# Windowed channel attention: both gate products of a pair of steps issued together ahead of an even step's value product, one in the pair banks and one in the score banks

## The chip, the cores and the metric

The kernel runs on one core of one Trainium2 chip, in one launch. The metric is device microseconds, the median of three runs. TensorE (PE) does the matrix products, VectorE (DVE) and ScalarE (ACT) read the results from the accumulation memory (PSUM), SyncE issues the transfers. All data are fp32.

## The reference

The input x is (4, 64, 128, 128). It is normalised in groups of two channels, and a block is added to it:

```python
qkv = einsum('bchw,oc->bohw', gn(x), w_qkv) + b_qkv      # 64 -> 192 channels
qkv = depthwise_conv_3x3(qkv, w_dw) + b_dw
# 8x8 windows: q, k, v of shape (windows, 4 heads, 16 channels, 64 pixels)
attn = softmax(einsum('nhcx,nhdx->nhcd', q, k) * temperature, axis=-1)
out  = einsum('nhcd,nhdx->nhcx', attn, v)
gate = gelu(einsum('nhcx,yx->nhcy', v, w_mlp) + b_mlp)
out  = einsum('bchw,oc->bohw', out * gate, w_proj) + b_proj
return x + out
```

Attention is over channels (a 16 x 16 table for each window and head), and the gate is a 64 x 64 product over the pixels of each window of v.

## The kernel before

The four images are two pairs; a pair's 2 x 64 channels fill the 128 partitions. A chunk is a band of 16 rows of one pair, that is 64 windows of 8 x 8 pixels (two rows of 16 windows for two images). There are 16 chunks. A chunk's windows are attended in four batches, so there are 64 steps; `a = i % 4` is the batch of step `i`. Step `i` belongs to chunk `i // 4`, and between its attention products PE does the work that prepares the next chunk, the filler units of `fillers(i)`:

- in a = 0 and a = 1 eight channel units each (`mix_channels`, L674, 8 records of MATMUL for a unit), which take the 10 x 10 patches through `w_qkv`;
- in a = 2 and a = 3 three depthwise units each (`depthwise`, L709, 64 records for a unit), numbered 0 to 5 here, which give q, k and v of 16 channels.

All units go through two PSUM buffers in turn (`work[0]`, `work[1]`, two banks each). ACT copies a unit out (L326), except depthwise unit 1, which DVE copies (L417). A unit can start only when the unit two before it is copied out. An fp32 product is two MATMUL records.

The attention of a step has these parts. On PE: `score` (L747, q times k), `gates` (L763, v times `w_mlp`, for a later step `j`), `turn_v` (L773, the transpose of v), `apply_probs` (L787, the value product), `project` (L796, of the step before). On DVE: `scores_up` (L511 to L518: mask, maximum, shift), `gate_up` (L525, gate product plus bias), `divide` and `turn` (L532 to L543), `mix` (L503, value product times gate), `residual` (L552). On ACT: `exponent` (L341), `v_up` (L347, copy of the transposed v) and `gelu` (L351). Exp and Gelu lie in different ACT tables, so each pair of gelus has a table load ahead of it, and an `exp_table` with another load (L356) behind it. Each engine runs its list in the order in which it is written; there is no scheduler.

The other four PSUM banks are `rest_ps`. `pair_ps` is its first two: the transposed v fills the first, `project` the second, and the value product the first halves of both. `score_ps` is its last two: scores in their first halves, and gate products in the second halves (`gate_ps`).

Before, `gates_in(i)` gives two gates to each odd step and none to an even one but the first. In an odd step one gate stands ahead of `project`, the other between two groups of filler units. `gate_up` of the first comes between `scores_up` and `divide` on DVE, that of the second after `residual`, behind `turn`. ACT's order in a = 3 is `exponent`, copy of unit 3, `v_up`, table load and `gelu`, copy of unit 4, `gelu`, copy of unit 5, `exp_table`. The first score of a chunk waits until units 4 and 5 are copied out (`qkv_of`), since it reads them.

Of the kernel before, what the change touches and what calls it, by code (L numbers as in the profile page):

```python
# [12 lines left out]
B, C, H, W = 4, 64, 128, 128  # L13
HEADS, WS = 4, 8
HW = WS * WS
# [12 lines left out]
BATCH = 4  # L28
BATCHES = COLS // BATCH
STEPS = CHUNKS * BATCHES  # L30
# [12 lines left out]
GATES = 3  # L43
# [42 lines left out]

def gates_in(i):

    return (0, 1) if i == 0 else (i + 1, i + 2) if i % 2 and i + 2 < STEPS else ()


def gelus_in(i):

    a = i % BATCHES
    return (0, 1) if i == 0 else (i, i + 1) if a == 2 else gates_in(i) if a == 3 else ()


def looks_until(i):
# [4 lines left out]
def build(nc, x, taps, hot, edges, weights, out):  # L103
    with ExitStack() as ctx:
# [45 lines left out]
        pair_ps = rest_ps[:, 0:2]  # L150
        turn_ps, proj_ps = pair_ps[:, 0], pair_ps[:, 1]
        score_ps = rest_ps[:, 2:4]
        gate_ps = score_ps[:, :, BATCH * C:]

        x_in = [sem(f"x_in{n}") for n in range(BANDS)]
        x_last = sem("x_last")
# [256 lines left out]
        def _(dve):  # L413
# [91 lines left out]
            def scores_up(i):  # L505

                dve.wait_ge(scores_done, i + 1)
                if i:
                    dve.wait_ge(probs_t_ready, i)
                over = [P, 2, BATCH, C]  # L510
                nc.vector.tensor_tensor(scores[:].rearrange("p (h g) d -> p h g d", h=2),  # L511
                                        score_ps[:, :, 0:BATCH * C].rearrange("p h (g d) -> p h g d", d=C),
                                        other_head.unsqueeze(1).unsqueeze(1).to_broadcast(over),
                                        ALU.add).then_inc(masked, 1)
                dve.wait_ge(masked, i + 1)
                nc.vector.tensor_reduce(neg_max[:], scores[:], AX_X, ALU.max, negate=True).then_inc(max_ready, 1)
                dve.wait_ge(max_ready, i + 1)
                nc.vector.tensor_tensor(scores[:], scores[:], neg_max[:].unsqueeze(2).to_broadcast([P, WIDE, C]),  # L518
                                        ALU.add).then_inc(shifted, 1)

            def gate_up(j):
                dve.wait_ge(gate_done, j + 1)
                if j >= GATES:
                    dve.wait_ge(proj_done, j - GATES + 1)
                nc.vector.tensor_tensor(  # L525
                    gate[:, j % GATES], gate_ps.rearrange("p b (g y) -> p b g y", y=HW),
                    b_mlp.unsqueeze(1).unsqueeze(1).to_broadcast([P, 2, BATCH, HW]), ALU.add).then_inc(gate_biased, 1)

            def divide(i):
# [55 lines left out]
            for i in range(STEPS):  # L585
                n, a = i // BATCHES + 1, i % BATCHES
                if i:
                    mix(i - 1)
                if (n, a) == (BANDS - 1, 1):
                    centre(1)  # L590
                if (n, a) == (BANDS - 1, 2):
                    variance(1)
                scores_up(i)
                now = gates_in(i)
                if now:
                    gate_up(now[0])
                elif i:
                    residual(i - 1)
                divide(i)
                turn(i)  # L600
                if now:
                    if i:
                        residual(i - 1)
                    gate_up(now[1])
                if n < CHUNKS and a == 2:
                    evacuate_dw(dve, copy, n, 1)
                if (n, a) == (BANDS - 1, 2):
                    normaliser(1)
                if a == 2 and n + 1 < CHUNKS:
                    pads(n + 1)  # L610
                    normalise(n + 1, 0)
                if a == 3 and n + 1 < CHUNKS:
                    normalise(n + 1, 1)
                for p in range(looks_until(i), looks_until(i + 1)):
                    look(p)
                if looks_until(i) < STATS <= looks_until(i + 1):
                    aggregate(1)
# [4 lines left out]
        def _(pe):  # L622
# [110 lines left out]
            def side(b, h):  # L733
                return slice((h ^ b) * HW, (h ^ b) * HW + HW)

            def score(i):

                if i:
                    pe.wait_ge(masked, i)
                    pe.wait_ge(gate_biased, max(j for m in range(i) for j in gates_in(m)) + 1)  # L740
                for g in range(BATCH):
                    q, k = windows(i, g)[:, 0], windows(i, g)[:, 1]
                    for b in range(2):
                        pair = slice(b * C, (b + 1) * C)
                        for h in range(2):
                            rows = slice(h * HW, (h + 1) * HW)
                            last = nc.tensor.matmul(score_ps[pair, h, g * C:(g + 1) * C], q[rows, pair], k[rows, pair],  # L747
                                                    start=True, stop=True)
                last.then_inc(scores_done, 1)

            def gates(j, i):

                pe.wait_ge(masked, i + 1)
                if j:
                    pe.wait_ge(gate_biased, j)
                if j // BATCHES > i // BATCHES:
                    wait_free(pe, ("dw", j // BATCHES, 0))
                    wait_free(pe, ("dw", j // BATCHES, 1))
                for g in range(BATCH):
                    for b in range(2):  # L760
                        for h in range(2):
                            rows = slice(h * HW, (h + 1) * HW)
                            last = nc.tensor.matmul(gate_ps[side(b, h), b, g * HW:(g + 1) * HW],  # L763
                                                    windows(j, g)[rows, 2, b * C:(b + 1) * C], mlp[rows],
                                                    start=True, stop=True)
                last.then_inc(gate_done, 1)

            def turn_v(i):

                if i:  # L770
                    pe.wait_ge(mixed_ready, i)
                for g in range(BATCH):
                    last = nc.tensor.transpose(pair_ps[:, 0, g * P:(g + 1) * P], windows(i, g)[:, 2], ident)  # L773
                last.then_inc(v_t_done, 1)

            def apply_probs(i):

                pe.wait_ge(v_t_ready, i + 1)
                pe.wait_ge(probs_t_ready, i + 1)
                if i:  # L780
                    pe.wait_ge(out_ready, i)
                for g in range(BATCH):
                    for h in range(2):
                        at = slice((2 * g + h) * HW, (2 * g + h + 1) * HW)
                        for b in range(2):
                            rows = slice(b * C, (b + 1) * C)
                            last = nc.tensor.matmul(pair_ps[side(b, h), b, g * HW:(g + 1) * HW],  # L787
                                                    probs_t[rows, h * BATCH + g, :], v_t[rows, at],
                                                    start=True, stop=True)
                last.then_inc(mix_done, 1)  # L790

            def project(i):

                pe.wait_ge(mixed_ready, i + 1)
                for b in range(2):
                    last = nc.tensor.matmul(proj_ps[:, b * 4 * HW:(b + 1) * 4 * HW], proj[:, b * P:(b + 1) * P],  # L796
                                            gate[:, i % GATES, b].rearrange("p g (r c) -> p r g c", c=WS),
                                            start=True, stop=True)
                last.then_inc(proj_done, 1)
# [14 lines left out]
                depthwise(0, v)  # L814
            for i in range(STEPS):
                units_now = fillers(i)
                now = gates_in(i)
                cut = (2, 4, 6) if i % BATCHES < 2 else (0, 1, 3) if i % BATCHES == 2 else (1, 2, 3)
                if i % BATCHES == 0:
                    qkv_of(i // BATCHES)  # L820
                if i == 0:
                    fill(units_now[:cut[0]])
                score(i)
                if i:
                    fill(units_now[:cut[0]])
                if now:
                    gates(now[0], i)
                if i:
                    project(i - 1)
                turn_v(i)  # L830
                fill(units_now[cut[0]:cut[1]])
                if now:
                    gates(now[1], i)
                fill(units_now[cut[1]:cut[2]])
                apply_probs(i)
                fill(units_now[cut[2]:])
            project(STEPS - 1)


# [82 lines left out]
```

## Time and profile before

| what | value |
|---|---|
| runs | 676.55, 679.05, 679.55 us; median 679.05 |
| profiled execution | span 680.0 us; no time of its own is given beside it, so it stands 0.95 us above the median |
| PE busy | 625.8 us, 92% of the span |
| DVE, ACT busy | 511.6 us (75%), 482.8 us (71%) |
| mean granted TensorE clock | 0.973 of full speed |

The profile shows one execution. A timeline row gives the start, the length and what an instruction (or a run of equal ones) is; a bracket at its end is the idle time of the engine ahead of it and what ended it. PE's products are pipelined, so a row's length runs into the next row: what a group costs is read from its start to the start of the next. A chunk of the middle takes 38.0 us.

### The profile page before, as it was taken

The page shows a single profiled execution, that of the slowest core. Times are in us where ns is not written, and L with a number is a line of the kernel's source. Part 1 is how long each engine was busy: PE and PEld are TensorE (multiplying, and loading weights), DVE is VectorE, ACT ScalarE, POOL GpSimd, SP SyncE. Part 2 cuts the span into 40 slices and gives each one's busy share as a digit, 9 for nine tenths or more (in the row PEclk, how much of TensorE's full clock was granted, in tenths as well). Part 3 has the DMA queues.
Part 4 walks back from the last instruction along what each step waited for, and adds up shares of the span by engine and source line. Part 5 has one row for each costly group of instructions (what it writes and reads, how often), then busy time and mean ns, then how long its engine had stood idle before and what let it go on. Part 6 is the DMA issues. An engine that isn't in the chain of part 4 may idle for free.

```text
span 680.0 us, 32438 instructions
## 1 busy us (share of the span) xinstructions
PE 625.8 (92%) x15044; PEld 549.1 (81%) x15044; DVE 511.6 (75%) x790; ACT 482.8 (71%) x631; POOL 0.3 (0%) x5
## 2 busy tenths in 40 slices
PE   3788799999999999999999999999999999999954
PEld 2687698888989898888989898888989798888843
DVE  4872688887888888786878676786868676876684
ACT  3652678787877778786877778786877778786722
POOL 0000000000000000000000000000000000000000
PEclk9997899999999999999999999999999999999975
DMA  9872115335171714132050504132150504112022
GB/s 363 263 217 72 33 50 166 110 86 208 33 232 49 234 59 149 66 102 93 8 191 5 195 4 142 60 94 106 29 173 4 198 3 152 44 50 80 4 82 44
DMA packets 29240, 72.28 MB, mean 106 GB/s; under 512 B 9801, under 2 KB 16329, under 8 KB 24233
## 3 DMA queue, kind: packets, MB, share of 16 engines
q1 hardware_dynamic: 28674, 68.57, 31.0%
q8 instruction: 118, 1.93, 1.2%
q10 hardware_dynamic: 432, 1.65, 0.7%
q14 instruction: 16, 0.13, 0.1%
HBM read 53.44 MB, written 16.78 MB: 103 GB/s over the span
## 4 chain that ended last, share of the span: by engine, by line
PE 87%; ACT 5%; DVE 3%; issue 2%; DMA 1%; ACTq 0%; DVEq 0%
PE unit_ps L709 28%; PE unit_ps L674 26%; PE rest_ps L796 10%; PE rest_ps L787 6%; PE rest_ps L763 6%; PE rest_ps L747 6%; PE rest_ps L773 4%; ACT z L326 2%; DMA patches<-in_hot 1%; ACT dw L326 1%; PE rest_ps L643 1%; PE rest_ps L674 1%; PE unit_ps L636 0%; DVE scores L511 0%; DVE scores L536 0%
## 5 line engine op out<-in xcount | busy, mean ns | idle before, releaser
L326 ACT ACTIVATE z<-unit_ps 100x768 f32<-100x768 f32 x244 | 184.9, 808 | 60.1 <-PE unit_ps L674 60.1
L674 PE MATMUL unit_ps<-consts,patches 64*100 64x192 f32 x1984 | 195.0, 336 | 8.6 <-ACT z L326 6.6
L709 PE MATMUL unit_ps<-z,dw 103*64 103x64 f32 (+2 forms) x6144 | 194.3, 224 | 3.0 <-issue 1.7
L709 PEld LDWEIGHTS unit_ps<-z,dw 103*64 103x64 f32 (+2 forms) x6144 | 185.5, 139 | 10.7 <-issue 8.6
L674 PEld LDWEIGHTS unit_ps<-consts,patches 64*100 64x100 f32 x1984 | 153.6, 164 | 25.8 <-ACT z L326 11.2
L326 ACT ACTIVATE qkv<-unit_ps 128x1024 f32<-128x1024 f32 x78 | 79.1, 1014 | 31.5 <-PE unit_ps L709 31.4
L511 DVE TENSOR_TENSOR scores<-rest_ps,consts 128x512 f32<-128x512 f32 x64 | 44.1, 689 | 51.6 <-PE rest_ps L747 51.6
L503 DVE TENSOR_TENSOR gate<-rest_ps,gate 128x512 f32<-128x512 f32 x64 | 44.1, 689 | 47.5 <-PE rest_ps L787 44.6
L796 PE MATMUL rest_ps<-gate,consts 128*128 128x256 f32 x256 | 75.1, 417 | 1.1 <-DVE gate L503 1.0
L347 ACT ACTIVATE v_t<-rest_ps 128x512 f32<-128x512 f32 x64 | 38.2, 597 | 40.5 <-PE rest_ps L773 38.9
L341 ACT ACTIVATE scores<-scores 128x512 f32<-128x512 f32 x64 | 40.4, 631 | 33.2 <-DVE scores L518 31.6
L787 PE MATMUL rest_ps<-v_t,probs_t 64*64 64x64 f32 x2048 | 45.5, 228 | 10.5 <-DVE probs_t L543 10.1
L525 DVE TENSOR_TENSOR gate<-rest_ps,consts 128x512 f32<-128x512 f32 x64 | 44.0, 687 | 14.4 <-PE rest_ps L763 14.0
L796 PEld LDWEIGHTS rest_ps<-gate,consts 128*128 128x128 f32 x256 | 44.9, 195 | 11.9 <-issue 3.5
L747 PE MATMUL rest_ps<-qkv 64*64 64x64 f32 x2048 | 45.4, 227 | 9.0 <-issue 9.0
L787 PEld LDWEIGHTS rest_ps<-v_t,probs_t 64*64 64x64 f32 x2048 | 36.7, 137 | 20.9 <-issue 18.8
L747 PEld LDWEIGHTS rest_ps<-qkv 64*64 64x64 f32 x2048 | 37.9, 138 | 18.1 <-issue 18.1
L552 DVE SCALAR_TENSOR_TENSOR staged<-rest_ps,consts,staged 128x512 f32<-128x512 f32 x64 | 46.7, 729 | 7.5 <-PE rest_ps L796 7.5
L543 DVE STREAM_TRANSPOSE probs_t<-scores 128x512 f32<-128x512 f32 x64 | 45.5, 712 | 2.2
L763 PE MATMUL rest_ps<-consts,qkv 64*64 64x64 f32 x2048 | 45.6, 228 | 1.6 <-DVE scores L511 1.6
L763 PEld LDWEIGHTS rest_ps<-consts,qkv 64*64 64x64 f32 x2048 | 36.7, 138 | 12.3 <-issue 8.2
L518 DVE TENSOR_TENSOR scores<-scores,neg_max 128x512 f32<-128x512 f32 x64 | 44.3, 692 | 2.2
(55 smaller groups left out, 530.5 us busy)
## 6 DMA issues: line engine op xcount, KB each, us to landing
staged<-in_x SPq DMA_DIRECT2D x17, 1024.0 KB, 4.9
out_y<-staged SPq DMA_DIRECT2D x15, 1024.0 KB, 5.4
T<-in_x SPq DMA_DIRECT2D x12, 1152.0 KB, 6.7
seen<-in_x SPq DMA_DIRECT2D x32, 256.0 KB, 2.9
qkv<-in_x SPq DMA_DIRECT2D x6, 1024.0 KB, 13.9
T<-in_x SPq DMA_DIRECT2D x3, 1088.0 KB, 6.7
staged<-in_x SPq DMA_DIRECT2D x2, 512.0 KB, 22.9
out_y<-staged SPq DMA_DIRECT2D x4, 256.0 KB, 3.0
```

What stands on the lines that cost most here:

```text
L326: return nc.scalar.activation(to, of, ACT.Copy)
L503: nc.vector.tensor_tensor(held, pair_ps[:, :, 0:BATCH * HW], held, ALU.mult).then_inc(mixed_ready, 1)
L511: nc.vector.tensor_tensor(scores[:].rearrange("p (h g) d -> p h g d", h=2), score_ps[:, :, 0:BATCH * C].rearrange("p h (g d) -> p h g d", ...
L518: nc.vector.tensor_tensor(scores[:], scores[:], neg_max[:].unsqueeze(2).to_broadcast([P, WIDE, C]), ALU.add).then_inc(shifted, 1)
L543: nc.vector.transpose(probs_t[:].rearrange("p w d -> p (w d)"), scores[:].rearrange("p w d -> p (w d)")).then_inc(probs_t_ready, 1)
L552: nc.vector.scalar_tensor_tensor(to, proj_ps.rearrange("p (r c) -> p r c", r=BAND), b_proj, to, op0=ALU.add, op1=ALU.add).then_inc(out_rea ...
L674: last = nc.tensor.matmul(to[0:NPATCH, t, b * QKV:(b + 1) * QKV], patches[image, b, g], w1[image], start=True, stop=True)
L709: last = nc.tensor.matmul(to[h * HW:(h + 1) * HW, m // 8, m % 8 * NW:(m % 8 + 1) * NW], dw[0:used, c, :], z[0:used, c, :], start=True, sto ...
L747: last = nc.tensor.matmul(score_ps[pair, h, g * C:(g + 1) * C], q[rows, pair], k[rows, pair], start=True, stop=True)
L763: last = nc.tensor.matmul(gate_ps[side(b, h), b, g * HW:(g + 1) * HW], windows(j, g)[rows, 2, b * C:(b + 1) * C], mlp[rows], start=True, s ...
L787: last = nc.tensor.matmul(pair_ps[side(b, h), b, g * HW:(g + 1) * HW], probs_t[rows, h * BATCH + g, :], v_t[rows, at], start=True, stop=True)
L796: last = nc.tensor.matmul(proj_ps[:, b * 4 * HW:(b + 1) * 4 * HW], proj[:, b * P:(b + 1) * P], gate[:, i % GATES, b].rearrange("p g (r c) ...
```

## The change

Each even step `i` gets the gates of steps `i + 2` and `i + 3`, both right ahead of its `apply_probs`; the odd steps get none. The even gate goes to the second halves of the pair banks, the odd one stays in the score banks. In the first step two more gates (0 and 1) stand ahead of its score. DVE keeps its two `gate_up` in the odd step: the first moves ahead of `scores_up`, the second behind `residual` and ahead of `divide`, so `residual` now stands ahead of `divide` in odd steps too. Gelus and copies on ACT stay where they were. Score's halves go to bank `h ^ b` instead of bank `h`, and the value product reads them so. Waits that are new or moved: the even gate waits for `out_ready` and `v_t_ready` of its step, the odd gate for `masked`, `apply_probs` for the even gate's end, `turn_v` and `project` of the next step for the even gate's `gate_up`; `score` no longer waits for `gate_up`.

```diff
 def gates_in(i):
-    return (0, 1) if i == 0 else (i + 1, i + 2) if i % 2 and i + 2 < STEPS else ()
+    return (i + 2, i + 3) if i % 2 == 0 and i + 2 < STEPS else ()

 def gelus_in(i):
     a = i % BATCHES
-    return (0, 1) if i == 0 else (i, i + 1) if a == 2 else gates_in(i) if a == 3 else ()
+    return (0, 1) if i == 0 else (i, i + 1) if a == 2 else gates_in(i - 1) if a == 3 else ()
...
-        gate_ps = score_ps[:, :, BATCH * C:]
+        gate_ps = [pair_ps[:, :, BATCH * HW:], score_ps[:, :, BATCH * C:]]
...
@@ DVE, each step @@
-                scores_up(i)
-                now = gates_in(i)
+                now = gates_in(i - 1) if i else (0, 1)
                 if now:
                     gate_up(now[0])
-                elif i:
+                scores_up(i)
+                if i:
                     residual(i - 1)
+                if now:
+                    gate_up(now[1])
                 divide(i)
                 turn(i)
-                if now:
-                    if i:
-                        residual(i - 1)
-                    gate_up(now[1])
...
@@ PE, score(i) @@
                     pe.wait_ge(masked, i)
-                    pe.wait_ge(gate_biased, max(j for m in range(i) for j in gates_in(m)) + 1)
...
-                            last = nc.tensor.matmul(score_ps[pair, h, g * C:(g + 1) * C], q[rows, pair], k[rows, pair],
+                            last = nc.tensor.matmul(score_ps[pair, h ^ b, g * C:(g + 1) * C], q[rows, pair], k[rows, pair],
...
@@ PE, gates(j, i) @@
-                pe.wait_ge(masked, i + 1)
-                if j:
-                    pe.wait_ge(gate_biased, j)
+                if j > 1:
+                    pe.wait_ge(gate_biased, j - 1)
+                if j % 2 == 0 and i:
+                    pe.wait_ge(out_ready, i)
+                if j % 2 == 0 and j:
+                    pe.wait_ge(v_t_ready, i + 1)
+                if j % 2 and j > 1:
+                    pe.wait_ge(masked, i + 1)
...
-                            last = nc.tensor.matmul(gate_ps[side(b, h), b, g * HW:(g + 1) * HW],
+                            last = nc.tensor.matmul(gate_ps[j % 2][side(b, h), b, g * HW:(g + 1) * HW],
...
@@ PE, turn_v(i) @@
+                for j in gates_in(i - 1)[:1] if i else (0,):
+                    pe.wait_ge(gate_biased, j + 1)
...
@@ PE, apply_probs(i) @@
+                for j in gates_in(i)[:1]:
+                    pe.wait_ge(gate_done, j + 1)
...
-                                                    probs_t[rows, h * BATCH + g, :], v_t[rows, at],
+                                                    probs_t[rows, (h ^ b) * BATCH + g, :], v_t[rows, at],
...
@@ PE, project(i) @@
+                for j in gates_in(i)[:1]:
+                    pe.wait_ge(gate_biased, j + 1)
...
@@ PE, each step @@
-                now = gates_in(i)
-                cut = (2, 4, 6) if i % BATCHES < 2 else (0, 1, 3) if i % BATCHES == 2 else (1, 2, 3)
+                cut = (2, 6) if i % BATCHES < 2 else (i % BATCHES - 2, 3)
...
                 if i == 0:
                     fill(units_now[:cut[0]])
+                    gates(0, 0)
+                    gates(1, 0)
                 score(i)
                 if i:
                     fill(units_now[:cut[0]])
-                if now:
-                    gates(now[0], i)
-                if i:
                     project(i - 1)
                 turn_v(i)
                 fill(units_now[cut[0]:cut[1]])
-                if now:
-                    gates(now[1], i)
-                fill(units_now[cut[1]:cut[2]])
+                for j in gates_in(i):
+                    gates(j, i)
                 apply_probs(i)
-                fill(units_now[cut[2]:])
+                fill(units_now[cut[1]:])
```

## Rows read from the trace of the kernel before

**Rows 1.** The page: the chain that ended last, by engine.
```profile
PE 87%; ACT 5%; DVE 3%; issue 2%; DMA 1%; ACTq 0%; DVEq 0%
```
**Rows 2.** Waits of PE: who for whom, total us, times, longest.
```profile
PE rest_ps L747 <- issue: 9.0, 15, 0.6
PE unit_ps L674 <- ACT z L326: 6.6, 15, 2.9
```
**Rows 3.** Timeline of PE over one chunk: start, length, instructions.
```profile
396.30 0.69 PE L747 MATMUL rest_ps<-qkv 64*64 64x64 f32 x32
...
404.17 0.69 PE L787 MATMUL rest_ps<-v_t,probs_t 64*64 64x64 f32 x32
404.69 0.65 PE L747 MATMUL rest_ps<-qkv 64*64 64x64 f32 x32
...
407.28 0.69 PE L763 MATMUL rest_ps<-consts,qkv 64*64 64x64 f32 x32
407.90 1.13 PE L796 MATMUL rest_ps<-gate,consts 128*128 128x256 f32 x4
...
414.06 0.69 PE L787 MATMUL rest_ps<-v_t,probs_t 64*64 64x64 f32 x32
415.36 0.70 PE L747 MATMUL rest_ps<-qkv 64*64 64x64 f32 x32 [0.61 <-issue]
...
418.96 1.55 PE L674 MATMUL unit_ps<-consts,patches 64*100 64x192 f32 x16
420.77 1.60 PE L674 MATMUL unit_ps<-consts,patches 64*100 64x192 f32 x16 [0.26 <-ACT z L326]
422.29 0.69 PE L787 MATMUL rest_ps<-v_t,probs_t 64*64 64x64 f32 x32
422.92 1.55 PE L674 MATMUL unit_ps<-consts,patches 64*100 64x192 f32 x16
424.40 0.69 PE L747 MATMUL rest_ps<-qkv 64*64 64x64 f32 x32
...
434.30 0.69 PE L747 MATMUL rest_ps<-qkv 64*64 64x64 f32 x32
```
**Rows 4.** Timeline of ACT over the same chunk.
```profile
407.70 0.63 ACT L341 ACTIVATE scores<-scores 128x512 f32<-128x512 f32 x1 [1.17 <-DVE scores L518]
408.24 1.01 ACT L326 ACTIVATE qkv<-unit_ps 128x1024 f32<-128x1024 f32 x1
409.51 0.60 ACT L347 ACTIVATE v_t<-rest_ps 128x512 f32<-128x512 f32 x1 [0.26 <-PE rest_ps L773]
...
411.96 1.01 ACT L326 ACTIVATE qkv<-unit_ps 128x1024 f32<-128x1024 f32 x1
412.90 0.63 ACT L351 ACTIVATE gate<-gate 128x512 f32<-128x512 f32 x1
414.23 1.02 ACT L326 ACTIVATE qkv<-unit_ps 128x1024 f32<-128x1024 f32 x1 [0.70 <-PE unit_ps L709]
...
419.90 1.51 ACT L326 ACTIVATE z<-unit_ps 100x768 f32<-100x768 f32 x2 [0.24 <-PE unit_ps L674]
```
**Rows 5.** Timeline of DVE over the same chunk.
```profile
402.49 1.23 DVE L417 COPY qkv<-unit_ps 128x1024 f32<-128x1024 f32 x1 [0.20 <-PE unit_ps L709]
...
404.93 0.69 DVE L503 TENSOR_TENSOR gate<-rest_ps,gate 128x512 f32<-128x512 f32 x1 [0.20 <-PE rest_ps L787]
405.54 0.68 DVE L511 TENSOR_TENSOR scores<-rest_ps,consts 128x512 f32<-128x512 f32 x1
...
418.63 0.75 DVE L552 SCALAR_TENSOR_TENSOR staged<-rest_ps,consts,staged 128x512 f32<-128x512 f32 x1 [0.38 <-PE rest_ps L796]
...
420.97 0.71 DVE L543 STREAM_TRANSPOSE probs_t<-scores 128x512 f32<-128x512 f32 x1
```
**Rows 6.** Timeline of PE at both ends of the span.
```profile
81.25 1.60 PE L674 MATMUL unit_ps<-consts,patches 64*100 64x192 f32 x16 [2.91 <-ACT z L326]
...
649.81 0.90 PE L787 MATMUL rest_ps<-v_t,probs_t 64*64 64x64 f32 x32 [3.90 <-DVE probs_t L543]
```

More of the change, by code:

```diff
@@ L525, in gate_up @@
                 nc.vector.tensor_tensor(
-                    gate[:, j % GATES], gate_ps.rearrange("p b (g y) -> p b g y", y=HW),
+                    gate[:, j % GATES], gate_ps[j % 2].rearrange("p b (g y) -> p b g y", y=HW),
                     b_mlp.unsqueeze(1).unsqueeze(1).to_broadcast([P, 2, BATCH, HW]), ALU.add).then_inc(gate_biased, 1)
```

## The prediction

> **What bounds the kernel now.** I read the page first: PE carries 87% of the chain that ended last [rows 1], so an edit counts by what it does to PE's list: what its groups cost, and where PE stands still. The list of PE's waits comes next. In the repeated part it has two: 0.6 us for the first score of each chunk, 15 times, and about 0.26 us for ACT's copies of channel units, 15 entries with the first chunk's long one among them [rows 2]. The first is labelled "issue", so I looked for its cause in the timelines: the score starts at 415.36 [rows 3], and ACT's copy of depthwise unit 5 ends at 414.23 + 1.02 = 415.25 [rows 4]. The score waits for that copy and starts 0.11 behind it. PE's timeline over a chunk then gives the lengths from score to score [rows 3]: a = 2 takes 8.39 (396.30 to 404.69), a = 3 10.67, a = 0 9.04, a = 1 9.90, in all 38.00. ACT and DVE are idle a quarter of the span, but both have chains inside a step that end close to PE's need; the change moves PE's cover away from some of them.
>
> **What a group of small products costs.** A gate between other work costs 0.62 (407.28 to 407.90), a value product between other work 0.63 (422.29 to 422.92). The one place where two such groups touch is the value product of a = 2 with the score behind it: 0.52 (404.17 to 404.69) [rows 3]. So a group that is followed by one of its own shape saves 0.10. An odd step loses two gates of 0.62, an even step gains two of 0.52: on PE's list alone the change saves 1.24 - 1.04 = 0.20 for each of about 30 pairs. Now step by step what the waits make of that. Times are counted from the step's score.
>
> **a = 0: +1.04.** The list up to the second filler group is as before, with its 0.33 of lost time inside the four channel units, which already stand in a row here: 418.96 to 420.77 is 1.81, where two units take 1.48 (422.92 to 424.40) [rows 3], because the third unit waits for the first's copy, at 419.90 [rows 4]. The gates come behind that, ahead of a value product that waited for nothing. No wait is there to hide them: the transposed probabilities are ready at 420.97 + 0.71 = 421.68 [rows 5], 0.6 ahead of the slot at 422.29. So 10.08. The value product's new wait for the even gate should be free: that gate is 0.69 long and starts 1.04 ahead of the slot, with the odd gate as 0.35 of cover.
>
> **a = 1: -0.76.** Without gates its list is that of a = 0 before, 9.04, with four channel units in a row and their 0.33: today the gate between them hides it. DVE's first `gate_up` stands ahead of `scores_up`, but the value product before started 2.11 ahead of this score (422.29 to 424.40), enough for `mix` and `gate_up` (0.61 each, start to start, by 404.93 to 405.54 [rows 5]). Its cost without that cover would be 0.61. Behind `scores_up` the `residual` starts 3.27 after the score and the transpose ends at 6.32, by a = 0's rows (418.63 and 421.68 against 415.36) [rows 5]; the second `gate_up` between them makes it 6.93, and with 0.1 for the handover the value product starts at 7.03, where its slot is 6.93 (422.29 - 415.36). So 9.14 in place of 9.90.
>
> **a = 2: +1.04.** Two gates at the end of three depthwise units. They read v of the next chunk and so wait for the copies of units 0 and 1; DVE's copy of unit 1 ends at 402.49 + 1.23 = 403.72 [rows 5], 0.45 ahead of the gates' slot at 404.17. If it were later, the value product would stand behind it too. 9.43 in place of 8.39.
>
> **a = 3: -0.51, not -1.24.** PE's own list shrinks: the value product's slot goes from 9.37 (414.06 - 404.69) to 8.13, and the next score's to 8.76. But that score waits for ACT's copy of unit 5, and ACT can't follow. Here value product and score touch, so DVE has no gap: `mix` starts at 404.93 and `scores_up` right behind it at 405.54 [rows 5]. A `gate_up` between them delays the scores' chain by 0.61. `exponent`, which waited for it at 3.01 (407.70), comes at 3.62. Behind it, by ACT's starts [rows 4]: copy of unit 3 after 0.54 (407.70 to 408.24), `v_up` after 0.94 more (as from 411.96 to 412.90), the second `gelu` 3.39 behind that (409.51 to 412.90, the table load among it), the copy of unit 5 another 0.54 on: 3.62 + 0.54 + 0.94 + 3.39 + 0.54 = 9.03. Before, that copy waited for PE until 9.54; now unit 5 is full at 9.54 - 1.24 = 8.30 and waits for ACT. It ends at 10.05, the score starts at 10.16, and PE stands still for 1.4 in place of 0.61. 10.16 in place of 10.67.
>
> **Sum.** A chunk: 1.04 - 0.76 + 1.04 - 0.51 = +0.81. Fourteen middle chunks give +11.3. In the first chunk the first step's extra gates, and the wait between its score and gate 0, lie ahead of a 2.91 wait for ACT [rows 6] that ends when gelus and tables are done, so they cost nothing, and the second step saves 0.76 as elsewhere; a = 2 and a = 3 give +0.53: together -0.2. The last chunk has no fillers: its gates fall into a wait of 3.90 for the probabilities [rows 6] and are free; in the step behind, the same DVE work stands ahead of the value product, which already waited for `residual`: 0. In all +11.1: 691.1 against the profiled span of 680.0, and 690.1 against the median of 679.05, which lies 0.95 below that span. I say 690.
>
> **Bounds.** An added group can cost 0.62 instead of 0.52 if the new wait for the even gate keeps the array from overlapping: +0.20 for each of 29 pairs, +5.8. Nothing in the rows puts it below 0.52. If the exponent of a = 3 is not delayed, 0.61 a chunk is not lost, -9.
>
> **A rule that speaks against the change** concerns score's new banks. Before, a bank of the scores was written from one row half of the array; now from both, into different halves of its partitions. The gates already write so, and a gate's 32 records are as long as a score's, 0.69 and 0.69 [rows 3], so I cost it at nothing. The Trainium skill, TensorEngine Tiling (Array Packing), Gotcha 1: PSUM Pressure, says that different row tiles cannot access one bank at the same time; by that rule taken plainly a score would take twice its time, some +40 in all, and this trace does not bear it out.
>
> **Rivals.**
> *PE's list alone sets the time* (faster). Then a = 1 and a = 3 keep their full -1.24 and the 0.61 wait stays: -0.40 a chunk, -5.6 over fourteen, about -1 in the first: 672. For it: PE's 87% of the chain, and the 0.10 saved at each place where groups touch. The Trainium skill, TensorEngine Tiling (Array Packing), Key Properties, says that a change of tiling mode drains the engine, and the change has fewer of them. Against it: ACT's chain. It decides at the copy of unit 5: that would have to end by 9.3 after a = 3's score, where ACT's rows give 10.05. Chance 0.10.
> *Most of ACT's delay doesn't come* (no change): the exponent of a = 3 stays at 3.01 because `mix` starts earlier, so that the copy ends at 9.44 and a = 3 takes 9.55. Then a chunk is +0.20: 682. Against it: `mix` and `scores_up` touch in the rows. Chance 0.12.
> *Touching groups save nothing here*: each added group at 0.62, as bounded above: 696. Chance 0.12.
> *Scores slow down by their banks*: 730. Chance 0.01.
>
> **Numbers.** The forecast has 0.65. Under 0.5% (3.4 us) this kernel can't be told from unchanged. Slower: 0.65 + 0.12 + 0.01 = 0.78; same 0.12; faster 0.10. The range leaves out the faster case, the banks' and the lowest part of the no-change case, and takes in the bound of 0.62 a group: 681 to 697.
>
> **What would show it.** In the profile of the changed kernel: the wait of the chunk's first score grows from 0.6 to about 1.4, and ACT's copy of unit 5 ends 0.1 ahead of it with no idle time in front; a = 1 shows the 1.81 between channel units, and perhaps a short wait of its value product for the transpose; a = 0 and a = 2 are longer by 1.0 each with gates at 0.52; a chunk takes 38.8. I am wrong if that score's wait stays at 0.6, if the gates cost less than 0.5 or as much as 0.62 each, or if the value product of an even step waits for the even gate's end.

## The result and the profile after

The changed kernel takes 690.85 us (median of four runs, 689.37 to 692.99), the kernel before 678.34 (676.55 to 679.55) beside it. The ratio is 1.0187, with a 95% interval of 1.016 to 1.0215: slower by 1.9%. The profiled execution has a span of 690.9 against 680.0. The changed kernel's profiled execution was timed at 692.99, 2.1 more than its span; by the same 2.1 the profiled execution before would stand near 682, above all four timed ones. So the two traces are 10.9 apart where the timed medians are 12.5 apart.

The page's chain that ended last, by engine, answers to [rows 1]:

```profile
PE 84%; ACT 6%; issue 5%; DVE 3%; DMA 1%; ACTq 0%; DVEq 0%
```

PE still carries the chain, but its share fell, and "issue", time in which PE waited for nothing that the profile names, went from 2% to 5%. PE's waits (who for whom, total us, times, longest) answer to [rows 2]:

```profile
PE rest_ps L744 <- issue: 17.7, 21, 1.4
PE unit_ps L672 <- ACT z L326: 11.0, 31, 2.1
PE unit_ps L707 <- issue: 6.6, 6, 1.9
PE rest_ps L765 <- ACT v_t L347: 2.0, 1, 2.0
```

L744 is the score, L672 the channel units, L707 the depthwise units, L765 the gates. The score's wait went from 9.0 us in 15 places to 17.7 in 21, the channel units' entries doubled from 15 to 31, and depthwise units wait in six places. The longest of these, 1.9, lies ahead of the first chunk, and the kernel before has one like it there (58.12, in the last section); the other five are new.

The middle fourteen chunks, from score to score, show the sum. Busy time of the engines (PE first) in that stretch, of before and then of after, in the view by windows:

```profile
109.60:643.73 534.13, 521.38 (x12997) 457.76 (x12997) 415.36 (x640) 413.68 (x549) 0.00 (x0) 1.00 0.31 99
```
```profile
107.11:653.04 545.93, 517.28 (x12997) 453.39 (x12997) 413.98 (x640) 411.16 (x549) 0.00 (x0) 1.00 0.30 97
```

With the same number of instructions and the clock at full in both, PE is busy for 4.1 us less and the stretch is 11.8 us longer. So PE stands still for 28.65 us in place of 12.75. The timeline of PE over one chunk shows where (a = 2 begins at 399.46, a = 3 at 408.78, where the score's first record stands among the last of the value product, a = 0 at 418.85, a = 1 at 428.84):

```profile
399.46 0.69 PE L744 MATMUL rest_ps<-qkv 64*64 64x64 f32 x32
...
407.33 1.16 PE L765 MATMUL rest_ps<-consts,qkv 64*64 64x64 f32 x64
408.31 0.65 PE L793 MATMUL rest_ps<-v_t,probs_t 64*64 64x64 f32 x30
408.78 0.22 PE L744 MATMUL rest_ps<-qkv 64*64 64x64 f32 x1
...
408.83 0.65 PE L744 MATMUL rest_ps<-qkv 64*64 64x64 f32 x30
409.42 2.08 PE L707 MATMUL unit_ps<-z,dw 103*64 103x64 f32 x64
411.43 1.13 PE L804 MATMUL rest_ps<-gate,consts 128*128 128x256 f32 x4
...
416.81 0.69 PE L793 MATMUL rest_ps<-v_t,probs_t 64*64 64x64 f32 x32
418.85 0.69 PE L744 MATMUL rest_ps<-qkv 64*64 64x64 f32 x32 [1.35 <-issue]
...
424.26 1.60 PE L672 MATMUL unit_ps<-consts,patches 64*100 64x192 f32 x16 [0.26 <-ACT z L326]
425.79 1.16 PE L765 MATMUL rest_ps<-consts,qkv 64*64 64x64 f32 x64
426.77 0.66 PE L793 MATMUL rest_ps<-v_t,probs_t 64*64 64x64 f32 x32
427.36 1.55 PE L672 MATMUL unit_ps<-consts,patches 64*100 64x192 f32 x16
428.84 0.69 PE L744 MATMUL rest_ps<-qkv 64*64 64x64 f32 x32
...
434.25 1.60 PE L672 MATMUL unit_ps<-consts,patches 64*100 64x192 f32 x16 [0.26 <-ACT z L326]
435.86 0.69 PE L793 MATMUL rest_ps<-v_t,probs_t 64*64 64x64 f32 x32
...
437.96 0.69 PE L744 MATMUL rest_ps<-qkv 64*64 64x64 f32 x32
```

The first score of the chunk now waits 1.35. The 0.26 between channel units, which stood only in a = 0, stands in a = 1 too (434.25). A pair of gates costs 0.98 (425.79 to 426.77) where two apart cost 1.24 [rows 3].

ACT's timeline ahead of that score, which answers to [rows 4]:

```profile
412.43 0.63 ACT L341 ACTIVATE scores<-scores 128x512 f32<-128x512 f32 x1 [2.75 <-DVE scores L518]
412.97 1.01 ACT L326 ACTIVATE qkv<-unit_ps 128x1024 f32<-128x1024 f32 x1
413.88 0.59 ACT L347 ACTIVATE v_t<-rest_ps 128x512 f32<-128x512 f32 x1
...
417.22 0.62 ACT L351 ACTIVATE gate<-gate 128x512 f32<-128x512 f32 x1
417.74 1.01 ACT L326 ACTIVATE qkv<-unit_ps 128x1024 f32<-128x1024 f32 x1
```

`exponent` starts 3.65 after the step's score, it waited 2.75 for DVE, and behind it ACT has no idle time up to the copy of unit 5. That copy ends at 418.75 and the score starts at 418.85. In all fourteen chunks the score starts 0.09 to 0.11 behind the end of that copy. DVE's timeline shows the delay, against [rows 5]: the first `gate_up` (L525) stands between `mix` and `scores_up`.

```profile
409.06 0.69 DVE L503 TENSOR_TENSOR gate<-rest_ps,gate 128x512 f32<-128x512 f32 x1 [1.17 <-PE rest_ps L793]
409.67 0.68 DVE L525 TENSOR_TENSOR gate<-rest_ps,consts 128x512 f32<-128x512 f32 x1
410.27 0.68 DVE L511 TENSOR_TENSOR scores<-rest_ps,consts 128x512 f32<-128x512 f32 x1
```

### The profile page after: what moved, and what is told of

Its sections match the earlier page's. It is cut to its first block, busy times and chain, and to the rows that moved or that the text cites. A ratio compares the mean times of both kernels' runs of the same rounds, so it can differ in the third digit from the quotient of the medians.

```text
span 690.9 us, 32466 instructions
## 1 busy us (share of the span) xinstructions
PE 617.4 (89%) x15044; PEld 541.4 (78%) x15044; DVE 509.6 (74%) x790; ACT 479.8 (69%) x631; POOL 0.3 (0%) x5
## 4 chain that ended last, share of the span: by engine, by line
PE 84%; ACT 6%; issue 5%; DVE 3%; DMA 1%; ACTq 0%; DVEq 0%
PE unit_ps L707 27%; PE unit_ps L672 24%; PE rest_ps L804 10%; PE rest_ps L744 6%; PE rest_ps L793 6%; PE rest_ps L765 5%; ACT z L326 4%; PE rest_ps L777 4%; DMA patches<-in_hot 1%; ACT dw L326 1%; PE rest_ps L641 1%; PE rest_ps L672 1%; PE unit_ps L634 0%; DVE neg_max L516 0%; DVE scores L511 0%
## 5 line engine op out<-in xcount | busy, mean ns | idle before, releaser
L672 PE MATMUL unit_ps<-consts,patches 64*100 64x192 f32 x1984 | 194.3, 335 | 13.1 <-ACT z L326 11.0
L707 PE MATMUL unit_ps<-z,dw 103*64 103x64 f32 (+2 forms) x6144 | 190.8, 223 | 7.8 <-issue 6.6
L707 PEld LDWEIGHTS unit_ps<-z,dw 103*64 103x64 f32 (+2 forms) x6144 | 183.7, 138 | 15.0 <-issue 14.0
L672 PEld LDWEIGHTS unit_ps<-consts,patches 64*100 64x100 f32 x1984 | 151.2, 163 | 35.9 <-ACT z L326 20.7
L744 PE MATMUL rest_ps<-qkv 64*64 64x64 f32 x2048 | 47.1, 227 | 17.7 <-issue 17.7
L744 PEld LDWEIGHTS rest_ps<-qkv 64*64 64x64 f32 x2048 | 38.9, 138 | 27.1 <-issue 27.1
L793 PEld LDWEIGHTS rest_ps<-v_t,probs_t 64*64 64x64 f32 x2048 | 38.8, 138 | 17.6 <-issue 16.3
L536 DVE TENSOR_TENSOR scores<-scores,inv_total 128x512 f32<-128x512 f32 x64 | 44.3, 692 | 2.2
L516 DVE TENSOR_REDUCE neg_max<-scores 128x8 f32<-128x512 f32 x64 | 43.9, 686 | 2.2
L525 DVE TENSOR_TENSOR gate<-rest_ps,consts 128x512 f32<-128x512 f32 x64 | 43.6, 682 | 2.3 <-PE rest_ps L765 2.3
```

The costliest lines, as they stand in the source:

```text
L536: nc.vector.tensor_tensor(scores[:], scores[:], inv_total[:].unsqueeze(2).to_broadcast([P, WIDE, C]), ALU.mult).then_inc(probs_ready, 1)
L672: last = nc.tensor.matmul(to[0:NPATCH, t, b * QKV:(b + 1) * QKV], patches[image, b, g], w1[image], start=True, stop=True)
L707: last = nc.tensor.matmul(to[h * HW:(h + 1) * HW, m // 8, m % 8 * NW:(m % 8 + 1) * NW], dw[0:used, c, :], z[0:used, c, :], start=True, sto ...
L744: last = nc.tensor.matmul(score_ps[pair, h ^ b, g * C:(g + 1) * C], q[rows, pair], k[rows, pair], start=True, stop=True)
```

## The experiments

All times of steps are read from score to score in PE's timelines, in a chunk without a wait in the middle of a group; "14 chunks" is from the second chunk's first score to the last chunk's. Ratios are to the kernel before, timed on the same chip in the same session (medians 677.98 to 678.72 in the three sessions of the runs below).

| kernel | a = 0 | a = 1 | a = 2 | a = 3 | chunk | 14 chunks | median us | ratio, 95% |
|---|---|---|---|---|---|---|---|---|
| before | 9.04 | 9.90 | 8.39 | 10.67 | 38.00 | 534.1 | 678.34 | |
| after | 9.99 | 9.12 | 9.32 | 10.04 | 38.47 | 545.9 | 690.85 | 1.0187 (1.016 to 1.0215) |
| copy5_first | 9.99 | 9.12 | 9.32 | 9.52 | 37.95 | 541.8 | 687.2 | 1.013 (1.0079 to 1.0182) |
| half_a0_pair | 9.99 | 9.12 | 8.39 | 10.67 | 38.17 | 538.0 | 684.95 | 1.0104 (1.0055 to 1.0153) |
| half_a2_pair | 9.04 | 9.91 | 9.32 | 10.04 | 38.31 | 542.4 | 688.3 | 1.0182 (1.0128 to 1.0236) |
| shifted_stream | 9.99 | 9.13 | 9.32 | 10.04 | 38.48 | 545.3 | 700.48 | 1.0325 (1.0262 to 1.0389) |
| gate_behind_unit5 | 9.44 | 9.90 | 8.39 | 10.19 | 37.92 | 534.3 | 677.3 | 0.9982 (0.9957 to 1.0006) |
| pair_in_odd | 9.04 | 9.75 | 8.39 | 10.51 | 37.69 | 529.9 | 676.04 | 0.9967 (0.994 to 0.9994) |
| unit_ahead | 8.43 | 9.91 | 8.39 | 10.82 | 37.55 | 527.6 | 671.36 | 0.9893 (0.9865 to 0.992) |
| pair_and_unit | 8.43 | 9.75 | 8.39 | 10.66 | 37.23 | 523.9 | 670.65 | 0.9887 (0.9856 to 0.9918) |

**copy5_first**: is ACT's copy of unit 5 what a chunk's first score waits for?

```diff
                 for j in now:
                     gelu(j)
                     if more and a == 3 and j == now[0]:
                         evacuate_dw(act, copy, n, 4)
-                if more and a == 3:
-                    evacuate_dw(act, copy, n, 5)
+                        evacuate_dw(act, copy, n, 5)
```

> The changed kernel with one edit on ACT: in a = 3 the copy of depthwise unit 5 stands ahead of the second gelu. Theory (the copy of unit 5, held up by ACT's chain, sets the first score of a chunk): the copy starts 0.52 earlier, the wait of that score falls from 1.35 to about 0.8, a = 3 goes from 10.05 to about 9.5, and the time falls by some 15 x 0.5 = 7 us, to about 683. Rival (PE's list and its supply of instructions alone set the time): no change, 691. A later loss is possible if the second gelu and the table load behind the copy delay the first channel units of a = 0; then a = 0 grows from 9.99.

ACT, and then PE, in its timelines:

```profile
530.20 1.92 ACT L326 ACTIVATE qkv<-unit_ps 128x1024 f32<-128x1024 f32 x2
532.00 0.63 ACT L351 ACTIVATE gate<-gate 128x512 f32<-128x512 f32 x1
```
```profile
532.21 0.69 PE L743 MATMUL rest_ps<-qkv 64*64 64x64 f32 x32 [0.81 <-issue]
```

The two copies run together and end at 532.12, the score follows at 532.21, its wait is 0.81, a = 3 is 9.52, and a = 0 does not grow. The fourteen chunks are 4.1 us shorter and not 14 x 0.52 = 7.3: in the chunks that wait in the middle of a group (below) part of the gain is lost. The rival, that PE's list and its supply of instructions alone set the time, is out by the step lengths. The total is weaker evidence: about 683 was expected and 687.2 measured, and the two kernels' ratios have intervals that overlap.

**half_a0_pair and half_a2_pair**: the change in two halves. Only one of the two pairs of a chunk moves, the other stays in the odd step, at its two places and in the score banks:

```diff
 def gates_in(i):
-    return (i + 2, i + 3) if i % 2 == 0 and i + 2 < STEPS else ()
+    return (i + 2, i + 3) if i % 4 == 0 and i + 2 < STEPS else ()
+
+def split_in(i):
+    return (i + 1, i + 2) if i % 4 == 3 and i + 2 < STEPS else ()
```

(for the second half `i % 4 == 2` and `i % 4 == 1`; PE and DVE issue the `split_in` gates as the kernel before does).

> Half of the change: the pair of gates that moved from a = 1 to a = 0 stays moved, the pair that moved from a = 3 to a = 2 goes back to its two places in a = 3 (both in the score banks, gate_up in the old order). Theory (the loss lies mostly where a = 3 can't give back what a = 2 pays, because ACT's chain is the longer one there): a = 2 back to 8.4 and a = 3 to 10.67, a = 0 and a = 1 at 9.99 and 9.12, a chunk about 38.2, in all 680 to 683. Rival (each moved pair costs the same): half of the 12 us, 684 to 685. If the stalls in the middle of groups come from four small groups in a row (two gates, value product, score), they are gone here.

> The other half of the change: the pair of gates that moved from a = 3 to a = 2 stays moved, the pair of a = 1 is back at its two places there. Theory (the two halves add up, and the four small groups in a row of a = 2 and a = 3 bring the waits for instructions with them): a = 0 and a = 1 at 9.04 and 9.90, a = 2 at 9.32 and a = 3 at 10.05 in chunks without such a wait, so a clean chunk is 38.3, and some 0.4 a chunk more for the waits: 685 to 688. Rival (the waits for instructions come from the number of instructions in a chunk alone): no idle time in the middle of a group, 682 to 683.

The step lengths are as expected to 0.05. The totals are not: 684.95 where 680 to 683 was expected and the rival had 684 to 685, and 688.3 where 685 to 688 was. The equal price that this rival asks for does not show in the traces all the same. Over the fourteen chunks the halves cost 3.9 and 8.2 us, together 12.1, where the whole costs 11.8: they add up, and the pair that left a = 3 is the dearer one. By the clean steps alone it would be 0.17 x 14 = 2.4 and 0.31 x 14 = 4.3. The rest is idle time in the middle of a group. The half of a = 0 has one such wait of 1.18 (in the score of a = 1 of one chunk), where no four small groups touch; the half of a = 2 has them in most chunks, as the changed kernel does.

**shifted_stream**: what are the waits in the middle of a group? In the changed kernel eleven scores or depthwise units stop halfway for 0.37 to 1.41 us, with all their semaphores long passed. They come in the chunks 0 and 1, 3 and 4, 6 and 7, 9 and 10, 12 and 13 (counted from 0), and in every third chunk at nearly the same record.

```diff
-            idle_products(24)
+            idle_products(4)
+            for _ in range(41):
+                nc.tensor.matmul(rest_ps[:, 0, 0:1], group_mean, w1[:, 0:1], start=True, stop=True)
```

> The changed kernel with 84 more PE instructions ahead of the first chunk (20 of the 24 idle products at the start are replaced by 41 one-column products; their result is not used). Nothing in the chunks changes. Theory (the idle times in the middle of a depthwise unit or a score, 0.4 to 1.4 us, are waits for PE's next 256 instructions): since a chunk is about 1880 instructions, a third of 256 more than a multiple, 84 more make chunk c stall as chunk c + 1 did. The stalls leave the chunks 1, 4, 7, 10, 13 and come in 2, 5, 8, 11, 14; total time as before within 2 us. Rival (they come from the chunk's own data, its transfers or its semaphores): they stay in the chunks 0 and 1, 3 and 4, 6 and 7, 9 and 10, 12 and 13.

A score of a = 3 in the changed kernel, in its chunk 10, and then one of this kernel, in its chunk 9:

```profile
486.70 0.55 PE L744 MATMUL rest_ps<-qkv 64*64 64x64 f32 x23
488.65 0.38 PE L744 MATMUL rest_ps<-qkv 64*64 64x64 f32 x9 [1.41 <-issue]
```
```profile
455.37 0.55 PE L744 MATMUL rest_ps<-qkv 64*64 64x64 f32 x23
456.70 0.38 PE L744 MATMUL rest_ps<-qkv 64*64 64x64 f32 x9 [0.79 <-issue]
```

Both stop behind record 23 of 32, one chunk earlier here. The waits left the chunks 4, 7, 10 and 13 and are in 2, 3, 5, 8, 9, 11, 12 and 14: they go by the position in PE's stream of instructions, not by what the chunk does. The part of the expectation on the total was wrong: the fourteen chunks take 545.3 (545.9 in the changed kernel), but the first score comes at 73.07 in place of 65.50, and the start ran at a lower clock. The view by windows of the stretch from 33 to 48 us (length, busy time of PE, PEld, DVE, ACT and POOL, then the granted clock, the DMA share and GB/s) shows a clock of 0.62 here, in the first fence, and of 1.00 in the changed kernel, in the second:

```profile
33.00:48.00 15.00, 14.30 (x87) 13.97 (x89) 5.77 (x16) 3.31 (x5) 0.00 (x0) 0.62 0.59 166
```
```profile
33.00:48.00 15.00, 13.09 (x142) 12.47 (x142) 11.67 (x21) 8.19 (x11) 0.00 (x0) 1.00 0.83 247
```

**gate_behind_unit5**: the kernel before, with work put between unit 5 and the score that waits for its copy.

```diff
-                cut = (2, 4, 6) if i % BATCHES < 2 else (0, 1, 3) if i % BATCHES == 2 else (1, 2, 3)
+                cut = (2, 4, 6) if i % BATCHES < 2 else (0, 1, 3) if i % BATCHES == 2 else (1, 3, 3)
```

and ACT's edit of copy5_first.

> The kernel before with two edits in a = 3: the second gate stands behind depthwise unit 5 instead of between units 4 and 5, and ACT copies unit 5 ahead of the second gelu. Theory (the first score of a chunk waits for the copy of unit 5, so work put between unit 5 and that score hides the copy, and units 4 and 5 and the gate and value product save 0.1 each where they touch): that wait falls from 0.6 to 0.1 or 0.2, a = 3 from 10.67 to about 9.95, the time by 15 x 0.7 = 10 us to about 668. Rival (the price of groups by their neighbours alone counts): 0.2 a chunk, 675.

The expected gain did not come: 677.3 where 668 was expected, and 675 by the rival. PE and DVE around the score:

```profile
450.57 0.69 PE L746 MATMUL rest_ps<-qkv 64*64 64x64 f32 x32 [0.44 <-DVE gate L524]
451.60 1.55 PE L673 MATMUL unit_ps<-consts,patches 64*100 64x192 f32 x16 [0.33 <-DVE patches L487]
```
```profile
449.74 0.69 DVE L524 TENSOR_TENSOR gate<-rest_ps,consts 128x512 f32<-128x512 f32 x1 [2.38 <-PE rest_ps L762]
450.35 1.10 DVE L487 TENSOR_SCALAR patches<-T,norm 128x1600 f32<-128x1600 f32 x1
```

The late gate makes a late `gate_up`. The score, which writes the same banks, waits 0.44 for it, and behind it on DVE stands the normalisation of the next patches, for which the first channel unit then waits 0.33. a = 3 gained 0.48 and a = 0 lost 0.40 (0.60 in the chunks 1 to 5). The cover has to be work that nobody behind the score waits for.

**pair_in_odd**: the touching pair in two pairs of banks, without losing the cover.

```diff
 def gates_in(i):
-    return (i + 2, i + 3) if i % 2 == 0 and i + 2 < STEPS else ()
+    return (i + 1, i + 2) if i % 2 and i + 2 < STEPS else ()
...
-                cut = (2, 6) if i % BATCHES < 2 else (i % BATCHES - 2, 3)
+                cut = ((2, 6, 6), (2, 4, 6), (0, 3, 3), (1, 2, 3))[i % BATCHES]
...
                 for j in gates_in(i):
                     gates(j, i)
+                fill(units_now[cut[1]:cut[2]])
                 apply_probs(i)
```

This diff is against the changed kernel and leaves out DVE's and ACT's new order and the semaphore waits that go with it.

> Both gates of a pair next to each other in two pairs of banks as in the change, but in the odd steps, where a wait or a gap stands: in a = 1 between the two groups of channel units ahead of the value product, in a = 3 between depthwise units 4 and 5. DVE's two gate_up follow the transpose, ACT loads the table for the gelus ahead of unit 4's copy and runs both gelus behind it, then copies unit 5. Theory (touching gates save 0.13 each, and the cover of a = 1 and a = 3 stays): a = 1 falls from 9.90 to 9.64, a = 3 from 10.67 to about 10.4, a chunk to 37.5, the time by 7 to 8 us to 670 to 672. Rival (the value product's wait for the first gate_up, or ACT's chain with both gelus ahead of unit 5, takes the saving back): 677 to 680.

PE in a = 1:

```profile
461.95 1.16 PE L768 MATMUL rest_ps<-consts,qkv 64*64 64x64 f32 x64
463.04 1.55 PE L674 MATMUL unit_ps<-consts,patches 64*100 64x192 f32 x16
```

The pair with other work behind it costs 1.09 and not 0.98, so it saves 0.15 against two apart; each of a = 1 and a = 3 falls by that. A chunk is 37.69, its chunks have no wait over 0.25 in the middle of a group, and the time is lower by 0.3%: 676.04, where 670 to 672 was expected and the rival had 677 to 680. I had the direction, but the size came out smaller, 0.31 in place of 0.5 in a chunk and some 2 us in place of 7 to 8 in the time: 0.13 for each of the two gates was wrong, since only the first of the pair touches one of its kind.

**unit_ahead**: the kernel before, with one channel unit in the wait of the chunk's first score.

```diff
+                ahead = 1 if i and i % BATCHES == 0 else 0
+                fill(units_now[:ahead])
                 if i % BATCHES == 0:
                     qkv_of(i // BATCHES)
...
                 if i:
-                    fill(units_now[:cut[0]])
+                    fill(units_now[ahead:cut[0]])
```

> The kernel before with one edit: at the start of a chunk (not the first) one channel unit stands ahead of the score instead of behind it. Nothing else moves. Theory (that score's wait of 0.6 is for ACT's copy of depthwise unit 5, and a channel unit, 0.74 long and in the other buffer, can run in it): the wait goes, the score starts 0.15 later than now, and a chunk falls from 38.00 to about 37.45, the time by 15 x 0.55 = 8 us to about 670. Rival (ACT's copies of the first channel units then come late, since its table load stands ahead of them, and the second unit or the value product waits in its place): 677 to 680.

```profile
406.28 0.69 PE L787 MATMUL rest_ps<-v_t,probs_t 64*64 64x64 f32 x32
406.90 0.90 PE L674 MATMUL unit_ps<-consts,patches 64*100 64x192 f32 x8
407.73 0.69 PE L747 MATMUL rest_ps<-qkv 64*64 64x64 f32 x32
408.36 0.90 PE L674 MATMUL unit_ps<-consts,patches 64*100 64x192 f32 x8
```

The wait is gone, a chunk is 37.55 (expected 37.45), and the time 671.36, 1.1% under the kernel before. This is the gain that neither the kernel before nor the change had.

**pair_and_unit**: both of these edits.

> The pair of gates together in the odd steps (as in pair_in_odd), and one channel unit ahead of a chunk's first score (as in unit_ahead). Theory (two separate effects, which add up): a chunk of about 37.15 (37.69 less 0.55), the time 665 to 668. Rival (both draw on the same slack of ACT at the end of a = 3): no more than the better of the two alone.

A chunk is 37.23, so the two gains add up (0.31 and 0.45 off 38.00). The median of 670.65 is 0.7 under unit_ahead's, with overlapping intervals. That misses the 665 to 668 that was expected and looks like the rival's "no more than the better of the two", though the chunk does not: the fourteen chunks take 523.9, 3.7 less than in unit_ahead. Whether the time follows the chunk stays open, for in the profiled execution, the slowest of its six, the first score came at 70.56 in place of 63.81.

## Why the prediction was right, point by point

The forecast was 690, the result 690.85 (+11.1 and +12.5 against the kernel before), and the theory of the steps is the one that the experiments leave standing. But the terms did not all have the size that they were given, and a wait that the prediction did not have makes up for it. That the total agrees to 1 us is luck in that part.

**Groups that touch.** Taken at 0.52 for each added gate; measured 0.98 for a pair and 0.59 for the value product behind it (425.79 to 427.36), so +0.95 in a = 0 and +0.93 in a = 2, where I had +1.04. A gate of the pair comes to 0.49: just under the 0.5 that I had named as a sign of being wrong, and under the 0.52 below which nothing in the rows was to put it. PE's busy time fell by 4.1 over 28 pairs, 0.15 a pair. The saving goes the way of the Trainium skill's rule on tiling modes (TensorEngine Tiling (Array Packing), Key Properties) that stood beside the rival. It is too small to set the time, and no run tells a drain from another cost of a change of shape.

**a = 1.** Forecast -0.76, measured -0.78, with the lost 0.33 between channel units where it was expected. The value product starts 7.02 after the score (428.84 to 435.86); 7.03 was forecast.

**a = 3.** Forecast 10.16, measured 10.04. In the chunk shown `exponent` is at 3.65 (forecast 3.62), the copy of unit 5 at 8.96 (9.03), the score's wait 1.35 (1.4). copy5_first shows that this copy decides.

**A chunk.** So a clean chunk is +0.47, not +0.81. Fourteen of them make 6.6 us. Yet the fourteen chunks cost 11.8, nearly the 11.3 of the forecast: the other 5.2 are the waits for instructions, which the prediction did not have. Two gates, a value product and a score in a row are four groups of 64 instructions in 2.1 us (407.33 to 409.42), and by the rows this outruns PE's supply. The eleven waits sum to 9.4 us, 8.1 of it in the fourteen chunks; part of that is not paid, since ACT catches up in the meantime and the next first score waits 0.6 again. The two errors, 4.7 too much on the clean chunk (2.8 of it on the groups, the rest on a = 3 and a = 1) and 5.2 too little on the supply, cancelled.

**Both ends.** I gave the first chunk -0.2 and the last 0. The second chunk's first score comes 2.5 earlier (107.11 against 109.60). Most of that looks like the clock of the execution: from 48 to 66 us the granted clock was 0.82 before and 1.00 after, and unit_ahead, whose program is the same as before up to its first score, reached that score 2.9 earlier than before did. The last chunk costs +1.6. It is 36.30 long before and 35.40 in gate_behind_unit5, which runs the same there, so such a difference carries an error of about 1. There the gates went into the wait for the probabilities as forecast, but what was moved had kept the engine active in the next step: PE then stood 4.02 and ran the step behind at the lower clock (0.50 from 668.0 to 671.3, where before had 1.00 from 657.0 to 663.7 in the same step). PE, and DVE in the same stretch:

```profile
667.30 0.69 PE L793 MATMUL rest_ps<-v_t,probs_t 64*64 64x64 f32 x32 [4.02 <-DVE probs_t L543]
667.79 1.03 PE L744 MATMUL rest_ps<-qkv 64*64 64x64 f32 x32
668.80 2.07 PE L804 MATMUL rest_ps<-gate,consts 128*128 128x256 f32 x4
```
```profile
672.78 0.69 DVE L532 TENSOR_REDUCE total<-scores 128x8 f32<-128x512 f32 x1 [1.09 <-ACT scores L341]
```

The projection takes 1.87 from start to start, 0.97 at full clock, the transpose of v behind it is late, ACT's copy of it stands ahead of `exponent`, and DVE waits 1.09 for that. The step (a = 2 of the last chunk) takes 8.25 to 8.54 in the four kernels that move the pair of a = 1 to a = 0, and 6.76 to 7.03 in the four that leave it at its two places, half_a2_pair and before among them. So the loss goes with that pair; that it is the clock's is read from the trace, and no run took the fall of the clock away.

**The banks.** A score with its new banks is 0.69 long and costs 0.63 (428.84 to 429.47), as before. The 40 us that I took from the Trainium skill's rule on row tiles (TensorEngine Tiling (Array Packing), Gotcha 1: PSUM Pressure) are not there.

**The rivals.** The faster one failed where it was said to decide, at the copy of unit 5. The one with no change needed an early `mix`; `mix`, `gate_up` and `scores_up` touch. 0.62 for each added group did not come: the value product does not wait for the even gate's end.

## What to carry to other kernels

Work that is moved pays in full in the step that it joins, where no wait there can take it, and is given back in the step that it leaves only down to that step's next longest chain; here a pair moved from a = 3 paid 0.93 and got back 0.63. Put movable work where the engine already stands, and make it work that nobody just behind it waits for: one channel unit in a wait of 0.6 gave 1.1%, a gate put ahead of that wait gave nothing. A forecast that comes out is still to be checked by its terms, since here two of some 5 us cancelled.

## What the runs showed of the hardware

PE's instructions arrive in packets, and a row of short products can outrun them. The page's row of that queue (packets, MB, share) is

```profile
q8 instruction: 118, 1.93, 1.2%
```

which is 16 KB a packet. PE issued 15,044 records of MATMUL and as many weight loads, 30,088 in all, so a packet holds about 255. The Trainium skill, Runtime: NRT & Kernel Launch, Instruction fetch mechanics, has blocks of 16 KiB, 256 instructions, that a sequencer fetches ahead; the rows agree with the size. It calls the cost of a block's edge mostly hidden. In the chunks of the kernel before it is hidden but for some 0.3 us (in a = 3 of chunk 14, which takes 11.03), and ahead of them PE waits 1.68 in a long row of depthwise units. Where 256 instructions went by in 2.1 us it was not hidden: waits of 0.37 to 1.41, at places that moved by one chunk when 84 instructions (32,466 to 32,550 in the page) were put ahead.

That each wait is for one such packet can be read from the traces in two ways. First, count PE's records in the order of time, weight loads and semaphore instructions among them: the record behind each of the eleven waits has a number that leaves 193 or 194 when divided by 256. So it is for all 52 waits of over 0.25 us in the middle of a score, a value product or a depthwise unit in the ten traces, the one of 1.68 included. Second, in all 52 PE goes on 1.19 to 1.60 us after a packet of this queue has landed. One of them: from 447 to 451 us the changed kernel has one packet (447.90 to 449.31), PE stops at 449.31 and goes on at 450.50. That packet, PE's row, and then the row of the kernel before ahead of its chunks:

```profile
q8 instruction: 1, 0.02, 2.2%
```
```profile
450.50 1.15 PE L707 MATMUL unit_ps<-z,dw 103*64 103x64 f32 x31 [1.19 <-issue]
```
```profile
58.12 2.14 PE L709 MATMUL unit_ps<-z,dw 106*64 106x64 f32 x58 [1.68 <-issue]
```

For ten of the eleven waits the 256 instructions ahead went by in 2.3 to 2.8 us; in the chunks of the kernel before no 256 took less than 3.05. The eleventh (195.71), and half_a0_pair's only one, which stands at the same record, came after longer; in the changed kernel it was 3.5, with the DMA engines' share at 0.96 ahead of its packet and 1.01 while it moved. Whether the other transfers held that packet up is not shown.

The clock at the start matters as much as any of these edits. With 41 one-column products in place of 20 full ones ahead of the first chunk, the first score came 7.6 us later, and the granted clock from 33 to 48 us was 0.62: a mean over its two levels of 1.2 and 2.4 GHz, so about three quarters of that stretch ran at the lower one. Both runs of that kernel were as slow (700.43 and 700.52), but only one was profiled. Kernels whose start was left alone differ too: before was granted 0.82 from 48 to 66 us and pair_and_unit 0.88, where the changed kernel had 1.00. So how much of the 7.6 is the edit's stays open.
